# Setup block rebuilt around the first LayerNorm, and weight preparation respread, in a Mamba plus FP4 feed-forward kernel

## Reference

```
mod = silu(c) @ wmod                      # six rows of 512: sa, ca, ga, sb, cb, gb
ga, gb = sign(g) * max(|g|, 0.25)
h = layernorm(x) * (1 + ca) + sa          # first half: Mamba
xz = h @ W_in.T;  xc, z = split(xz)       # 1024 + 1024 channels
xc = silu(causal_conv4(xc))
dlt, B, C = split(xc @ W_xproj.T)         # 32 + 16 + 16
delta = softplus(dlt @ W_dt.T + b_dt)
h_t = exp(delta*A) * h_(t-1) + delta*B*xc ;  y = sum_n h*C + xc*D
x = x + ga * ((y * silu(z)) @ W_out.T)
h = layernorm(x) * (1 + cb) + sb          # second half: feed-forward, FP4 blocks of 16
x = x + gb * fp4_linear(silu(fp4_linear(h, w_gate)) * fp4_linear(h, w_up), w_down)
```

## Time and profile before

| | |
|---|---|
| median of 3 executions | 5404.15 us (5402.94 to 5407.81) |
| profiled execution | 5406.93 us, its span 5405.0 us |
| busy: PE, VectorE, ScalarE, GpSimd | 4828.6 (89%), 4896.0 (91%), 3550.8 (66%), 3942.6 (73%) us |
| end of the setup block | 24.5 us |
| first amax of the weight preparation | 35.2 us |
| `x_low` | 150.0 us |
| first scan of chunk 0 | 171.2 us |
| HBM traffic | 698.05 MB read, 43.26 MB written |

### The profile page before, as it was taken

One profiled execution on the slowest core, in us unless ns is written; L12 is line 12 of the kernel. 1 busy time (PEld: TensorE's weight loads), 2 busy tenths in 40 slices (PEclk: granted clock), 3 DMA queues, 4 the chain that ended last, 5 costly groups with the idle time before them and its releaser, 6 DMA issues. The chain is left out here.

```text
span 5405.0 us, 78213 instructions
## 1 busy us (share of the span) xinstructions
PE 4828.6 (89%) x21996; PEld 3327.3 (62%) x21996; DVE 4896.0 (91%) x4117; ACT 3550.8 (66%) x7762; POOL 3942.6 (73%) x1844
## 2 busy tenths in 40 slices
PE   7589888898888989889898898976899999999999
PEld 3355555555555555555555555554788888888888
DVE  7899999999999999989999999998788888888887
ACT  2678778778777777878877778775444444444442
POOL 5899999999999999989999999997223232322221
PEclk9799999999999999999999999997999999999999
DMA  6455555555555555555655555555110101010100
GB/s 224 150 188 179 188 184 181 190 180 187 191 169 191 181 183 185 179 183 177 192 185 175 190 180 187 183 168 174 47 35 29 35 29 35 29 35 29 35 29 28
DMA packets 399483, 745.67 MB, mean 138 GB/s; under 512 B 44067, under 2 KB 44195, under 8 KB 398982
## 3 DMA queue, kind: packets, MB, share of 16 engines
q1 hardware_dynamic: 394758, 724.18, 41.0%
q0 software_dynamic: 4352, 17.30, 0.9%
HBM read 698.05 MB, written 43.26 MB: 137 GB/s over the span
## 5 line engine op out<-in xcount | busy, mean ns | idle before, releaser
L659 POOL TENSOR_TENSOR slot<-du,b_row 128x1024 f32<-128x1024 f32 x1024 | 2396.8, 2364 | 8.7 <-ACT lead_decay L836 5.3
L1016 DVE TENSOR_TENSOR_SCAN decays<-decays,state,slot 128x1024 f32<-128x1024 f32 x656 | 1539.2, 2346 | 57.4 <-ACT slot L891 56.8
L882 ACT ACTIVATE decays<-delta,rate 128x512 f32<-128x512 f32 x2048 | 1327.0, 680 | 23.8
L1143 PEld LDWEIGHTS y_ps<-ident,slot 128*128 128x128 f32 x8192 | 969.8, 146 | 354.5 <-issue 239.0
L1143 PE MATMUL y_ps<-ident,slot 128*128 128x128 f32 x8192 | 1060.3, 281 | 118.1 <-POOL slot L666 76.5
L1068 PE MATMUL work_ps<-h_t,win 128*128 128x512 f32 x2048 | 966.8, 617 | 89.7 <-ACT zs L760 37.1
L666 POOL TENSOR_TENSOR slot<-slot,c_row 128x1024 f32<-128x1024 f32 x368 | 868.8, 2361 | 171.2 <-ACT state L869 165.5
L1515 POOL TENSOR_TENSOR hq<-hid,qinv 128x1408 f32<-128x1408 f32 x63 | 163.4, 2593 | 1049.9 <-DVE qinv L1541 1049.9
L1016 DVE TENSOR_TENSOR_SCAN slot<-decays,state,slot 128x1024 f32<-128x1024 f32 x368 | 857.3, 2339 | 46.6 <-ACT slot L891 46.6
L1022 DVE TENSOR_TENSOR slot<-decays,c_row 128x1024 f32<-128x1024 f32 x656 | 801.9, 1222 | 57.0 <-DVE decays L1016 3.7
L1068 PEld LDWEIGHTS work_ps<-h_t,win 128*128 128x128 f32 x2048 | 387.4, 197 | 539.8 <-issue 431.2
(11 more groups left out here) (268 smaller groups left out, 8038.3 us busy)
## 6 DMA issues: line engine op xcount, KB each, us to landing
b_row<-b_c_rows SPq DMA_DIRECT2D x1024, 256.0 KB, 3.8
c_row<-b_c_rows SPq DMA_DIRECT2D x1024, 256.0 KB, 3.6
win<-in_w_in SPq DMA_DIRECT2D x256, 256.0 KB, 4.3
xt<-in_x SPq DMA_DIRECT2D x16, 1024.0 KB, 7.5
xr<-in_x SPq DMA_DIRECT2D x64, 256.0 KB, 4.1
x_after_mamba<-xr SPq DMA_DIRECT2D x64, 256.0 KB, 4.1
xa<-x_after_mamba SPq DMA_DIRECT2D x64, 256.0 KB, 2.8
xres<-x_after_mamba SPq DMA_DIRECT2D x64, 256.0 KB, 2.6
```

The lines of the kernel that those rows point to most:

```text
L659: pool.tensor_tensor(slot[:, u % SLOTS, :, :], du[:, p % 2, :, :], two(b_row[:, u % BC_RING, :]), ALU.mult).then_inc(S["ub_ready"], 1)
L882: act.activation(decay[u % 2][:, i, :], delta[:, p % 2, i, :], ACT.Exp, scale=rate[:, 2 * p + i, n:n + 1]).then_inc(S["decay_ready"], 1)
L1016: dve.tensor_tensor_scan(d if u in DVE_C else h, d, h, state[:, 2 * p, n:n + 1], ALU.mult, ALU.add).then_inc(S["scan_done"], 1)
L1143: op = pe.matmul(y_ps[i][:, s, :], slot[:, u % SLOTS, i, s * P:(s + 1) * P], ident[:, :], is_transpose=True, start=False, stop=(n == N - 1 ...
```

## The change

- **Setup block.** The loads of x and of the convolution taps come ahead of `wmod`, and `wmod` comes as two halves, placed in `wout`'s room. The first LayerNorm (sums, squares, seed on ScalarE; four small products on GpSimd; four applies on ScalarE) runs in this block. sa and ca are made as rows: for each, `c_act` is stationary and a half of `wmod` moves (four products of 512 columns), ScalarE copies the row out and TensorE turns it into columns with four products of one row. ScalarE's order is silu, sums, squares, seed, row copy 0, applies 0 and 1, row copy 1, applies 2 and 3, exp(A_log). VectorE waits for that exp before `rate` and the split of `wdt`.
- **Loads in the setup block's SP queue.** After the ones above SP issues, still before the block's end, the first four `win`, the loads of groups 0 to 5 and two of the four vectors; in all 12.8 MB by the shapes (before: 3.9 MB in this block). The other two vectors and `wout` follow in the main block. GpSimd issues no loads any more.
- **Stores and later loads.** SP stores groups 0 to 4 and loads groups 6 to 9 between its `load_win` steps (`turn_over`); GpSimd stores groups 5 to 9.
- **Vectors.** Order mix, gate, scale, shift, each by eight products in a row: mix after the last h, gate after c1, the columns of gate after c3, scale after d0, shift after d1. ScalarE copies scale after sp_exp 0 and shift after sp_exp 1. `signed` for gate now works on 128x4 columns (four instructions) ahead of group 6; for mix it runs ahead of group 2.
- **First convolutions.** `conv_out` of chunk 0 applies silu on the way out of PSUM; `silu_x` of chunk 0 is left with a semaphore increment.
- **wout.** GpSimd's four products stand between groups 3 to 6.
- **Last groups.** `prepare` on VectorE and GpSimd stops short; prep_of(9) stands after `x_low`, prep_round(8) after sp_out 0, prep_round(9) after sp_out 1; GpSimd's product for group 8 stands before du, that for group 9 after `times_b` of units 0 and 1. `times_b` of unit 0 waits for the store of group 8, that of unit 6 for group 9.

The core of the diff (the setup block's new parts first):

```diff
+                LOADS = [(c_loaded, c_in[:, :], c_vec), (x_first, taps[:, :, :], w_conv),
+                         (x_first, xt[:, :, :], x[0:T, :].rearrange("(s p) d -> p s d", p=P))]
+                LOADS += [(mod_loaded[i], wmod[i], w_mod[:, :, i * DM:(i + 1) * DM]) for i in range(2)]
+                REST = [(rate[:, :, :], a_log), (wx[:, :, :], w_x), (dskip[:, :], d_skip)]
...
+                        for done, dst, src in LOADS:
+                            sp.dma_start(dst, src).then_inc(done, 16)
+                        for i in range(WIN_RING):
+                            load_first_win(sp, i)
+                        prep_load(sp, 0)
+                        load_vector(sp, 0)
+                        prep_load(sp, 1)
+                        load_vector(sp, 1)
+                        for g in range(2, PREP_RING):
+                            prep_load(sp, g)
...
+                        act.wait_ge(row_done, 1)
+                        act.activation(mod_row[:, 0, :], row_ps[0:1, 0, :], ACT.Copy).then_inc(row_copied, 1)
+                        act.wait_ge(first_newton, 5)
+                        for s in range(TILES):
+                            if s == 2:
+                                act.wait_ge(row_done, 2)
+                                act.activation(mod_row[:, 1, :], row_ps[0:1, 1, :], ACT.Copy).then_inc(row_copied, 1)
+                            act.activation(xt[:, s, :], xt[:, s, :], ACT.Identity, bias=neg_mr[:, s:s + 1], scale=rstd[:, s:s + 1])
+                        act.wait_ge(rest_loaded, 16 * len(REST))
+                        act.activation(rate[:, :, :], rate[:, :, :], ACT.Exp).then_inc(a_exp, 1)
...
+            SP_SAVES = {5: (0,), 7: (1,), 9: (2,), 10: (3,), 11: (4,)}
...
+                    def turn_over(i):
+                        if i in SP_SAVES:
+                            for r in SP_SAVES[i]:
+                                prep_save(sp, r)
+                                if r + PREP_RING < len(PREP):
+                                    sp.wait_ge(prep_saved[r], 16 * len(PREP[r]))
+                                    prep_load(sp, r + PREP_RING)
...
-                        act.activation(xc[c.parity][:, j, :], work_ps[b][:, :], ACT.Copy).then_inc(bank_free[b], 1)
+                        act.activation(xc[c.parity][:, j, :], work_ps[b][:, :],
+                                       ACT.Silu if c.reg is None and c.off == 0 else ACT.Copy).then_inc(bank_free[b], 1)
...
+                                    elif (step, arg) == ("sp_exp", 0):
+                                        row_out(2)
+                                    elif (step, arg) == ("sp_exp", 1):
+                                        row_out(3)
...
+                    def signed_gate():
+                        dve.wait_ge(col_out, 1)
+                        chain(dve.scalar_tensor_tensor(gb_mag[:, :], gb_raw[:, :], -1.0, gb_raw[:, :], ALU.mult, ALU.max), 1)
+                        chain(dve.tensor_scalar(gb_mag[:, :], gb_mag[:, :], 0.25, None, ALU.max), 2)
+                        chain(dve.tensor_scalar(gb_raw[:, :], gb_raw[:, :], 0.0, 2.0, ALU.is_ge, ALU.mult), 3)
+                        chain(dve.scalar_tensor_tensor(gb_col[:, :], gb_raw[:, :], -1.0, gb_mag[:, :], ALU.add, ALU.mult), 4)
...
                     def prepare():
+                        for g in range(LAST):
+                            if g == 2:
+                                signed_mix()
+                            if PREP[g][0][0] is w_down and PREP[g - 1][0][0] is not w_down:
+                                signed_gate()
+                            prep_of(g)
                             if g >= 1:
                                 prep_round(g - 1)
+                    def prep_between(step, arg):
+                        if step == "x_low":
+                            prep_of(LAST)
+                        elif (step, arg) == ("sp_out", 0):
+                            prep_round(LAST - 1)
+                        elif (step, arg) == ("sp_out", 1):
+                            prep_round(LAST)
...
+                                    if (step, arg) == last_h:
+                                        row_mm(0)
+                                    elif (step, arg) == ("c", 1):
+                                        row_mm(1)
+                                    elif (step, arg) == ("c", 3):
+                                        gate_columns()
+                                    elif (step, arg) == ("d", 0):
+                                        row_mm(2)
+                                    elif (step, arg) == ("d", 1):
+                                        row_mm(3)
```

More of the change, by code:

```diff
@@ new lines, in late_saves @@
+            def late_saves(r):
+                return 16 * sum(len(PREP[i]) for i in range(PREP_RING, r + 1))
+            VECTORS = (("mix", 2, du[:, :, :, :].rearrange("p a b t -> p (a b) t")),
+                       ("gate", 5, delta[:, :, :, :].rearrange("p a b t -> p (a b) t")),
+                       ("scale", 4, c_row[:, :, :]), ("shift", 3, xr[:, :, :]))
+            win_loaded = [sem(f"win_loaded{i}") for i in range(WIN_RING)]
+            vec_loaded = [sem(f"vec_loaded{i}") for i in range(len(VECTORS))]
@@ L685, in _ @@
                     pool.memset(halo[:, :, :], 0.0).then_inc(S["cleared"], 1)
-                    pool.memset(const[:, :], 1.5).then_inc(S["cleared"], 1)
-                    for g in range(2):
-                        prep_load(pool, g)
-                    pool.wait_ge(S["cleared"], 5)
+                    pool.wait_ge(S["cleared"], 4)
                     all_chunks(pool, body)
@@ L844, in row_out @@
                         name = VECTORS[i][0]
-                        if name == "shift":
+                        if name == "gate":
+                            act.activation(gate_row, src, ACT.Copy).then_inc(rows_out, 1)
+                        elif name == "shift":
                             act.activation(ffn_rows[:, 0, :], src, ACT.Copy).then_inc(rows_out, 1)
@@ L993, in prepare @@
[L993 to L1002 removed]
+                            dve.wait_ge(own, n)
@@ L1180, in _, with row_mm @@
-                    passed = [0]
+                    def row_mm(i):
+                        wait(pe, rows_out, i)
+                        if i >= 2:
+                            pe.wait_ge(col_out, 1)
+                        pe.wait_ge(vec_loaded[i], 16)
+                        for k in range(KT):
+                            op = pe.matmul(y_ps[1][:, :, :].rearrange("p s q -> p (s q)"), c_wide[:, k, :], VECTORS[i][2][:, k, :],
+                                           start=(k == 0), stop=(k == KT - 1))
+                        op.then_inc(rows_done, 1)
@@ L1181, in _, with gate_columns @@
+                    def gate_columns():
+                        pe.wait_ge(rows_out, 2)
+                        for m in range(KT):
+                            op = pe.matmul(y_ps[1][:, 0, m:m + 1], gate_row[0:1, m * P:(m + 1) * P], one[0:1, 0:1],
+                                           start=True, stop=True)
+                        op.then_inc(col_done, 1)
                     all_chunks(pe, body)
```

400 lines of the change are left out of this document (208 added, 192 removed).

## The result

The changed kernel takes 5362.86 us (median of three, 5358.39 to 5366.99) where the kernel before takes 5404.15: a ratio of 0.9923, 95% interval 0.991 to 0.9937, faster by 41 us. Forecast were 22 us and a range that ends at 5371; the time lies outside it, on the fast side. On a second chip, beside experiments e10 to e12, the same kernel came to 5371.69 against 5404.3 (0.9941, 0.9927 to 0.9954), 33 us. So the gain is 33 to 41 us, the forecast's 22 and some 11 to 19 more.

What follows compares the result with a forecast made beforehand. VectorE's preparation was taken to bound the start up to `x_low`, the loop (VectorE and GpSimd nearly always busy) staying unchanged. Terms -7.4 - 22.4 + 7.0 + 0.5 = -22.3 us take 5404.15 to 5382, range 5371 to 5396.

Steps and rivals of the forecast that it cites:

- The step that failed: Chunk loop: nothing repeated is edited, so an earlier first scan brings the end forward by as much.
- the slower loop: Rival, chunk loop: engines enter chunk 0 offset differently, each chunk pays; 2.5 us per chunk gives 5421; chance 0.09.
- End of the block: Setup block: SP's load issues end last, at about 27.2 us (bounds 24.8 to 29.7), 2.7 later than before.
- The term of -7.4: Start of the preparation: VectorE's first amax at 27.8 instead of 35.24 us, -7.4 us.
- Amax to `x_low`: VectorE's preparation from first amax to `x_low`: 92.4 instead of 114.8 us, -22.4, VectorE still setting it.
- The gate: Signing the gate on VectorE before `x_low`: 4.5 us beside a GpSimd product instead of 4.9, -0.4; lower bound 0.6.
- the scale line of group 7: VectorE's line 967 before `x_low`: no collision for group 7, GpSimd being busy; sum over groups 6 to 8 unchanged.
- The three preparation steps that leave that stretch: prep_of(9), prep_round(8) and prep_round(9) leave VectorE's path to `x_low`: 5.5 + 4.95 + 4.95 = 15.4 us.
- TensorE's path to `x_low`: TensorE's x ends at 111.5, `x_out` at 113.5, so VectorE is last by some 7 us.
- `x_low` to scan 0: Chain behind `x_low`, 21.2 us before: scale and shift rows add 7.0 us, moved VectorE work hides; 2.4 smaller if clock holds.
- the thin one: Between `x_low` and scan 0: prep_round(9) ends at + 25.6, decays due at + 25.8; without this cover it costs 5 us.
- Sum of the start: Everything up to the first scans: -7.4 - 22.4 + 7.0 + 0.5 = -22.3 us, 0.41%.

Runs made afterwards that it cites:

- e10: The changed kernel with the loop over the middle chunks written out, so no engine jumps: 5357.48 us, 0.9912 of the kernel before.
- e12: The changed kernel with loads of groups 3 to 5 issued in the main block and the chunk loop written out: 5350.66 us, 0.9900 of the kernel before.
- e1: The kernel before with 16 idle semaphore increments in TensorE's queue ahead of the chunk loop: 5385.59 us, 0.9959 of the kernel before.
- e2: The changed kernel with 66 idle semaphore increments on TensorE, putting its loop at the earlier kernel's place: 5386.98 us, 0.9967 of the kernel before.
- e11: The kernel before with the loop over the middle chunks written out: 5373.87 us, 0.9945 of the kernel before.
- e6: The changed kernel with loads of groups 3 to 5 issued by SP in the main block, not the setup block: 5364.96 us, 0.9925 of the kernel before.
- e8: The changed kernel with the last group's scales and last two roundings back ahead of `x_low`: 5380.27 us, 0.9952 of the kernel before.
- e7: The changed kernel with TensorE's scale row behind x instead of d0, its copy behind `x_out`: 5369.37 us, 0.9938 of the kernel before.
- e9: The changed kernel itself, run again on one chip beside the written-out kernels: 5371.69 us, 0.9941 of the kernel before.

## Why the prediction was wrong, point by point

- **The step that failed** is in the first paragraph: "the change edits nothing that the loop repeats, so whatever brings the first scan forward brings the end forward by as much". The loop's work is the same, but its code lies at another place, and in the profiled pair the loop became 31.1 us shorter. e1 moves nothing but TensorE's code and makes the kernel before 21.7 us faster, 16.5 of them at unit 2; e2 puts 18.9 us on the changed kernel, 8.7 of them at unit 2; e10 and e11 take the jump away, and both kernels' loops become equal to 2.4 us. The forecast had put this term at nothing.
- **The rival that came nearest**, the slower loop, named a mechanism (phase of the engines) and one sign only. With the phase changed and the jump gone, the loops are equal: that mechanism is worth no more than the 2.4 us between two traces. The rows for the other one were at hand: 148 us of idle VectorE in the loop were counted as "already in it", though 24 us of them sat at unit 2 of five chunks, each behind a jump.
- **End of the block**: 29.9, just past the upper bound of 29.7, instead of 27.2. The computing engines were done at 24.4 (24.8 forecast). SP's issues took 1.0 to 2.8 us each from 11.05 us on, the last one 0.64, and ended at 29.53. The miss has two parts of about equal size. The transfers ran at 369 GB/s between 5 and 29.53 us, not at the 398 of one window of 5 us, so the 9.1 MB had moved at 28.1 instead of 26.9. And when the last issue was through, 12.8 - 9.65 = 3.2 MB stood in the queue, not 3.7 (4.1 when it first held back, at 11.05). The term of -7.4 was -4.7. SP as the last was right, and e6 shows its price, 5.4 us at the first amax.
- **Amax to `x_low`**: 95.1 instead of 92.4. No w_down wait is left (7.7 forecast). The gate took 4.2 us (4.5 forecast), 3.54 of them for one line of four columns beside a GpSimd product of 93.16 to 96.84; the same kind of line took 0.17 just before. The Trainium skill ("SBUF — State Buffer", Who interferes with whom) has a `tensor_scalar` in a two-port mode and a GpSimd instruction exclude each other for the whole instruction, the first to issue winning; by these rows the excluding holds for 128x4 too. The excess is the scale line of group 7: 3.47 instead of 0.27. I had GpSimd busy with its `wout` product and the store; the `wout` product was over at 105.0, GpSimd issued the store from 108.80 on and began its next product at 110.09, and the line lasted from 109.30 until 112.77, past that product. It had started 0.79 us ahead of the product, so who came first did not decide here, or the store's issue held it already; no run tells which.
- **The three preparation steps that leave that stretch**: 15.4 forecast, 13.1 in e8, where the scale line met no product.
- **TensorE's path to `x_low`**: x ended at 118.5 instead of 111.5, `x_out` at 119.7 instead of 113.5. The block's end gives 2.7 us of this. From i0 to z0 TensorE took 71.4 us, not 66.4: the three vectors were taken off with their whole length, but their products had stood where TensorE would have waited for ScalarE's copies, and eight such waits of 0.7 to 0.8 us came to light. It cost nothing, since VectorE was still last by 5.9 us (7 forecast).
- **`x_low` to scan 0**: 26.2 instead of 28.2. The two rows cost 5.0, not 7.0, since the clock held better (0.89 against 0.82 in the earlier trace rows; the first row's eight products took 4.95 us). The other cover was the thin one: prep_of(9), costed at nothing, held VectorE until 132.0, when ScalarE's scale copy ended at 132.7, and with the row gone it is what sets d1 (e7).
- **Sum of the start**: -22.3 forecast, -19.4 in the profiled pair. Over all kernels scan 0 came at 167.6, 169.4 and 171.2 with the start of before and at 151.6 to 154.0 with that of after (155.7 in e2; e6 to e8 and e12 have another start), so 17 us are nearer than 19.
- **The rest of the 48.8 us between the two profiled spans** is the loop's 31.1: -21.2 at unit 2 (TensorE's place), +7.7 at unit 63 (GpSimd's place), -12.3 at unit 60, -5.8 elsewhere and +0.5 in the smallest distances; 1.7 us are given back behind it. Most of the 12.3 were luck of that execution: e9, the same kernel, has 15.0 at unit 60, 2.6 less than before.

Open are why the rest of the kernel costs 5 us more in e10 to e12, and what decides in which chunks unit 60 waits. That another start of the loop on ScalarE, VectorE or SP would matter as well was not tried.

## What to carry to other kernels

An edit ahead of a loop moves the loop's code, and each jump back then costs more or less: before a gain or loss of some tenths of a per cent is put down to the order of the work, compare the units behind and ahead of the jump, and run the kernel with a few idle instructions in front of the loop, or with the loop written out. In a stretch where two engines' work runs side by side, neither length is "hidden": cost the stretch for each engine alone and take the longer. Work taken off an engine gives back its length less the waits that it had covered. A setup block ends with its last DMA issue, so only the loads that it or the next few us need belong in it.

The fastest version is e12, 5350.66 us, 1.0% below the kernel before: late loads and the loop written out.

## What was not expected of the hardware

A jump back stops an engine even when nothing waits: TensorE 2.3 to 4.2 us from its last weight load to the next at each of five jumps, in every kernel with a loop, 16 KB of code arriving per packet. In the kernel before the second packet lands 6.5 to 8.5 us behind the branch. There and in e2, where TensorE runs only two weight loads behind the first stop, it then stands 2.7 to 4.3 us more.

Unit 60 waits come in steps, 1.4 to 1.8 or about 3 us, in some chunks of every kernel, jump or none. Windows of the changed kernel (PE busy, then the granted clock, DMA share, GB/s) around unit 60 of chunk 0, which waits, and of chunk 2, which doesn't, with the product of TensorE in each:

```profile
350.00:362.00 12.00, 8.66 (x35) 0.86 0.63 210
...
792.00:804.00 12.00, 10.33 (x43) 1.00 0.64 216
```
```profile
355.26 0.80 PE L1198 MATMUL work_ps<-dt_parts,wdt 98*128 98x512 f32 x1 [3.34 <-DVE delta L1030]
355.85 4.86 PE L1176 MATMUL work_ps<-h_t,win 128*128 128x512 f32 x8
...
797.48 0.51 PE L1198 MATMUL work_ps<-dt_parts,wdt 98*128 98x512 f32 x1 [1.67 <-DVE delta L1030]
797.82 3.60 PE L1176 MATMUL work_ps<-h_t,win 128*128 128x512 f32 x8
```

After 3.34 us of idle TensorE the eight products took 4.86 us, with a granted clock of 0.86 in that window, so part of them at 1.2 GHz; after 1.67 us of idle the clock was 1.00, 2.4 GHz, and they took 3.60. The same holds at this place in all 14 traces, 15 chunks each. In the 106 chunks without the wait TensorE stood idle for 1.62 to 1.76 us and the products took 3.60. In the 104 with it the idle time was 3.32 to 3.34 us; the products took 4.76 to 5.30 us in 89 of them, where the scan waits 1.4 to 1.8 us, and 6.37 to 6.45 in 15, where it waits 3.0 to 3.2. So the waits at unit 60 go with products at the lower clock behind the longer idle time; why TensorE's earlier work ends 1.7 us sooner in some chunks is not shown. Over the traces these waits sum to 5.3 to 19.2 us; between the two of the same kernel (after and e9) they make 9.7 of the 14.1 us by which the loops differ.
